# Recurrence of a decoder layer: another order of work on all engines, three pairs in flight, TensorE's program written out

## What is computed

```python
q = (x @ Wq).reshape(b, s, H, HD)
k = (x @ Wk).reshape(b, s, H, HD)
v = (x @ Wv).reshape(b, s, H, HD)
fg = jax.nn.sigmoid(x @ Wf + bf).reshape(b, s, H, HD)
...
state = state * gt[..., None] + vt[..., None] * kt[..., None, :]
out_t = jnp.einsum('bhij,bhj->bhi', state, qt)
```

## Time and profile before

| what | before |
|---|---|
| median of 3 runs | 2023.63 us (2019.81 to 2026.11) |
| the profiled execution: its own time | 2018.74 us |
| its span | 2016.6 us |
| TensorE busy in the span | 1864.5 us (92%) |
| VectorE, ScalarE, GpSimd busy | 1593.3, 1221.4, 390.4 us |
| mean granted clock of TensorE | 0.977 |
| the recurrence (to the first work of the next part) | about 755 us of the span |

### The profile page before, as it was taken

How to read it: one execution, slowest core, us unless ns; L and a number is a source line. 1 busy time by engine, 2 the same in 40 slices (tenths; PEclk the granted TensorE clock), 3 DMA queues, 4 the chain that set the end, 5 groups by cost and what they waited for, 6 DMA issues and landing times. The chain is left out here.

```text
span 2016.6 us, 71020 instructions
## 1 busy us (share of the span) xinstructions
PE 1864.5 (92%) x28151; PEld 1307.0 (65%) x28151; DVE 1593.3 (79%) x2870; ACT 1221.4 (61%) x2047; POOL 390.4 (19%) x516
## 2 busy tenths in 40 slices
PE   6999999999999977999999999999599988799798
PEld 4666666666666665888888888887344433344687
DVE  6777777777777775888888888887466799998897
ACT  4444554444445434777777777777355666688565
POOL 1111111211111121223232323232100222100121
PEclk9999999999999989999999999999699999999899
DMA  4001100110011001111111111110188788599574
GB/s 126 24 24 29 30 24 24 29 30 24 24 27 32 19 19 63 34 48 32 46 33 46 36 42 38 40 41 7 40 273 267 272 314 312 188 402 409 184 271 148
DMA packets 121324, 205.24 MB, mean 102 GB/s; under 512 B 44851, under 2 KB 98358, under 8 KB 121142
## 3 DMA queue, kind: packets, MB, share of 16 engines
q1 hardware_dynamic: 121142, 202.43, 29.4%
HBM read 108.01 MB, written 85.98 MB: 96 GB/s over the span
## 5 line engine op out<-in xcount | busy, mean ns | idle before, releaser
L1483 PE MATMUL ff_twin<-ff_xq,w_uh 128*128 (+1 forms) x1152 | 346.0, 382 | 40.0 <-DVE ff_top L1852 25.7
L1483 PEld LDWEIGHTS ff_twin<-ff_xq,w_uh 128*128 128x128 f16 x1152 | 110.4, 98 | 188.9 <-issue 43.2
L1483 PE MATMUL ff_twin<-ff_xq,w_ul 128*128 (+1 forms) x576 | 219.9, 382 | 0.0
L1214 DVE TENSOR_REDUCE mneg<-att_s 128x4 f32<-128x512 f32 x256 | 158.8, 683 | 31.3 <-PE att_s L977 31.3
L545 ACT ACTIVATE x<-rec_e,rec_hidden 128x512 f32<-128x512 f32 x256 | 155.8, 702 | 35.1 <-PE rec_e L380 35.1
L661 DVE TENSOR_TENSOR x<-rec_x,rec_until 128x512 f32<-128x512 f32 x256 | 158.7, 681 | 17.2 <-PE rec_x L364 17.2
L392 PE MATMUL rec_x<-x 32*32 32x64 f32 x8192 | 146.4, 219 | 14.9 <-DVE x L661 9.5
L392 PEld LDWEIGHTS rec_x<-x 32*32 32x32 f32 x8192 | 125.4, 107 | 51.4 <-issue 51.3
L288 POOL TENSOR_TENSOR rec_o<-rec_tmp 128x512 f32<-128x512 f32 x32 | 41.1, 1283 | 571.6 <-DVE rec_tmp L714 571.6
L1129 ACT ACTIVATE att_e<-att_s 128x512 f32<-128x512 f32 x256 | 132.2, 612 | 25.4 <-PE att_s L1011 25.4
L349 PE MATMUL rec_f<-rec_xT,w_rec 128*128 128x256 f32 x512 | 137.3, 402 | 0.8 <-ACT rec_v L527 0.8
(11 more groups left out here) (244 smaller groups left out, 4363.3 us busy)
## 6 DMA issues: line engine op xcount, KB each, us to landing
raw_scratch<-ff_out SPq DMA_DIRECT2D x32, 768.0 KB, 3.5
ff_in<-raw_scratch SPq DMA_DIRECT2D x32, 768.0 KB, 5.9
gate_scratch<-ff_out SPq DMA_DIRECT2D x28, 768.0 KB, 3.5
ff_in<-gate_scratch SPq DMA_DIRECT2D x28, 768.0 KB, 10.2
product_scratch<-ff_out SPq DMA_DIRECT2D x28, 768.0 KB, 9.7
ff_out<-product_scratch SPq DMA_DIRECT2D x28, 768.0 KB, 5.9
att_x<-in_x SPq DMA_DIRECT2D x32, 256.0 KB, 2.7
att_ctx<-in_ctx SPq DMA_DIRECT2D x32, 256.0 KB, 3.0
```

The lines of the kernel that those rows point to most:

```text
L1214: V.tensor_reduce(mneg[:, 4 * j:4 * j + 4], X[j].rearrange("p (h k) -> p h k", h=4), AX.X, ALU.max, negate=True).then_inc(q["s_taken"], 1)
L1483: m = T.matmul(bank_.rearrange("p (b n) -> p b n", b=BT), weights(wp, kc, a, c), tile[:, xp, :, kc], start=(i == 0), stop=(i == len(terms) ...
```

## The change

The recurrence's programs are written in another order on TensorE, ScalarE and VectorE. Each has now one `step` over the pairs prev, now and next_. TensorE's 34 steps are all written out, without a loop, so that its waits are on constants; ScalarE and VectorE keep a loop over two pairs. On TensorE `scores(., 0)` moves up into the step of its own pair, groups of small tiles stand next to each other (`inside` 0 and 1; `inside` 2 and half of `across_half`; a quarter part, `inside` 3, the other quarter part), `exponents` 3 and 4 stand together before the queries, and `value_gate` takes sequence 1 first. On VectorE `quarter_out` stands before `weighted(., 0)` and `half_out` behind it, and both `floor`s stand together. On ScalarE the queries' copies move behind the exponentials of k = 2, and the last two exponentials stand between the logarithm and its rounding. At the start the first `value_gate` waits for two weights, not for four; `sums` comes first on VectorE; the search for the scales is cut in three parts, of which `weigh_down` (which waits for three weight loads) stands before the first `split`. The functions keep their instructions; `across` is now `keys` and `queries`.

```diff
-    TURNS = 6
...
+        class Pair:
+            def __init__(self, j, c):
+                self.r, self.s, self.turn = 2 * j + c, c % 2, j + c // 2
+                self.first = isinstance(j, int) and c == 0
...
-                def products(p, n, s, so, front, back):
...
-                def pieces(p, s, before, front, back, more):
...
+                def step(at):
+                    prev, now, next_ = at(-1), at(0), at(1)
+                    if now:
+                        queries(now)
+                    if prev:
+                        scores(prev, 1)
+                    if now:
+                        keys(now, 0)
+                    if prev:
+                        inside(prev, 0)
+                        inside(prev, 1)
+                    if now:
+                        keys(now, 1)
+                        exponents(now, 0)
+                    if prev:
+                        inside(prev, 2)
+                        across_half(prev, 0)
+                    if now:
+                        exponents(now, 1)
+                    if next_:
+                        turn(next_)
+                    if now:
+                        exponents(now, 2)
+                    if prev:
+                        across_quarter(prev, 0)
+                        inside(prev, 3)
+                        across_quarter(prev, 1)
+                    if next_:
+                        value_gate(next_, 1)
+                    if prev:
+                        across_half(prev, 1)
+                    if next_:
+                        value_gate(next_, 0)
+                    if now:
+                        scores(now, 0)
+                        exponents(now, 3)
+                        exponents(now, 4)
                 pe.wait_ge(qw["ident_set"], 2)
...
-                with pe.Fori(0, (NP - 2) // TURNS) as j:
-                    for u in range(TURNS):
-                        p, s = TURNS * j + 1 + u, (1 + u) % 2
-                        pieces(p, s, TURNS // 2 * j + (1 + u) // 2, True, True, True)
-                        products(p + 1, p, 1 - s, s, True, True)
-                pieces(NP - 1, 1, (NP - 2) // 2, True, True, False)
-                products(NP, NP - 1, 0, 1, False, True)
-                pieces(NP, 0, NP // 2, False, True, False)
+                for p in range(-1, NP + 1):
+                    step(near(0, p))
...
+                def step(at):
+                    now, next_ = at(0), at(1)
+                    if now:
+                        keys_out(now)
+                        exps(now, 0)
+                    if next_:
+                        turned(next_)
+                    if now:
+                        exps(now, 1)
+                        exps(now, 2)
+                        queries_out(now)
+                    if next_:
+                        values_out(next_, 1)
+                        values_out(next_, 0)
+                        gate_exp(next_)
+                        gate_log(next_)
+                    if now:
+                        exps(now, 3)
+                        exps(now, 4)
+                    if next_:
+                        gate_high(next_)
...
+                def step(at):
+                    prev, now, next_ = at(-1), at(0), at(1)
+                    if prev:
+                        quarter_out(prev)
+                    if now:
+                        weighted(now, 0)
+                    if prev:
+                        half_out(prev)
+                    if next_:
+                        floor(next_, 1)
+                        floor(next_, 0)
+                        if next_.first:
+                            weigh_down()
+                    if now:
+                        scores_out(now, 0)
+                    if prev:
+                        total(prev)
+                    if now:
+                        scores_out(now, 1)
+                    if next_:
+                        split(next_)
+                        if next_.first:
+                            weigh_up()
+                    if now:
+                        weighted(now, 1)
                         for k in range(4):
-                            inside_out(n, so, k)
...
+                            inside_out(now, k)
+                        if now.first:
+                            weigh()```

TensorE, in the middle of the recurrence. First the place from the second scores to the first exponents. rec_x are the banks X, x with a source x is `inside`, rec_f the projections, rec_e `exponents`; a REGISTER_ALU or ISA row computes the number to wait for. Before:

```order
L364 MATMUL rec_x<-rec_qm,rec_kT 128x256 x8
L347 REGISTER_ALU
L349 MATMUL rec_f<-rec_xT,w_rec 128x256 x2
L386 REGISTER_ALU
L387 REGISTER_ALU
L392 MATMUL rec_x<-x 32x64 x32
L349 MATMUL rec_f<-rec_xT,w_rec 128x256 x2
L387 REGISTER_ALU
L392 MATMUL rec_x<-x 32x64 x32
L69 REGISTER_ALU
L380 MATMUL rec_e<-rec_nh,rec_sums_of 128x256
```

More of the change, by code:

```diff
@@ L165, in recurrence_block @@
         q = {n: sem("rec_" + n) for n in names}
-        names = "ident_set w_loaded bf_loaded raw_loaded rest_loaded part all chain weighed rounded turned copied high split cleared".split()
+        names = "ident_set w_loaded qk_loaded bf_loaded raw_loaded rest_loaded part all chain weighed rounded turned copied high split cleared".split()
         qw = {n: sem("weights_" + n) for n in names}
@@ L170, in blocks_of, with near, at @@
             return flat.rearrange("p (n q) -> p n q", q=QBLOCK)
-        def steps(eng, step):
-            step(0, 0, 0, True, False)
-            with eng.Fori(0, (NP - 2) // 2) as j:
-                for u in range(2):
-                    step(2 * j + 1 + u, (1 + u) % 2, j + u, True, True)
-            step(NP - 1, 1, (NP - 2) // 2, True, True)
-            step(NP, 0, NP // 2, False, True)
+        class Pair:
+            def __init__(self, j, c):
+                self.r, self.s, self.turn = 2 * j + c, c % 2, j + c // 2
+                self.first = isinstance(j, int) and c == 0
+        def near(j, u):
+            def at(k):
+                if isinstance(j, int) and not 0 <= u + k < NP:
+                    return None
+                return Pair(j, u + k)
+            return at
         def rows(j):
@@ L456, in pieces @@
-                def pieces(p, s, before, front, back, more):
-                    n, so = p - 1, 1 - s
-                    if back:
-                        inside(n, so, 0)
-                    if front:
-                        across(p, 1, F[0], 1, 1, q["k_made"])
-                    if back:
-                        inside(n, so, 1)
-                    if front:
-                        exponents(p, s, 0)
-                    if back:
-                        inside(n, so, 2)
-                    if front:
-                        exponents(p, s, 1)
-                    if more:
-                        turn(p + 1, so, before + s)
-                    if back:
-                        inside(n, so, 3)
-                    if front:
-                        exponents(p, s, 2)
-                    if back:
-                        across_half(n, 0)
-                    if more:
-                        value_gate(p + 1, 0)
-                    if back:
-                        across_half(n, 1)
-                    if front:
-                        exponents(p, s, 3)
-                    if back:
-                        across_quarter(n, 0)
-                    if front:
-                        exponents(p, s, 4)
-                    if back:
-                        across_quarter(n, 1)
-                    if more:
-                        value_gate(p + 1, 1)
@@ L517, in turned, with values_out @@
                 def turned(p):
-                    act.wait_ge(q["x_made"], p + 1)
+                    act.wait_ge(q["x_made"], p.r + 1)
                     A.activation(xT.rearrange("p k n -> p (k n)"), F[0][:], ACT.Copy).then_inc(q["xT_ready"], 1)
-                def step(p, s, before, front, back):
-                    if not front:
-                        return
-                    act.wait_ge(q["w_ready"], 2 * p) if not isinstance(p, int) or p else None
-                    for b in range(2):
-                        act.wait_ge(q["z_ready"], 2 * p + b + 1)
-                        A.activation(v[:, s, b * D:(b + 1) * D], F[1 - b][:, 0:D], ACT.Copy).then_inc(q["v_ready"], 1)
+                def values_out(p, b):
+                    if b == 1:
+                        wait_if(act, q["w_ready"], 2 * p.r - 2)
+                    act.wait_ge(q["z_ready"], 2 * p.r + 2 - b)
+                    A.activation(v[:, p.s, b * D:(b + 1) * D], F[1 - b][:, 0:D], ACT.Copy).then_inc(q["v_ready"], 1)
@@ new lines, in exps @@
+                def exps(p, k):
+                    if k == 0:
+                        wait_if(act, q["o_taken"], TAKES * (p.r - 1))
+                    act.wait_ge(q["e_made"], NE * p.r + k + 1)
+                    for asks, r in USES[k]:
```

(22 more changed lines are left out.)

255 lines of the change are left out of this document (111 added, 144 removed).

## The result

The changed kernel takes 2074.4 us (median of 4 runs, 2065.7 to 2077.9) against 2023.1 us: the ratio of the recorded runs is 1.0244 [1.0229, 1.0259] (the two medians alone give 1.0253), slower by 2.4%. The forecast was 2006 us. Its profiled execution, the shortest of the four, has a span of 2063.6 us, 47.0 us more than before.

What follows compares the result with a forecast made beforehand. TensorE was taken to bound the recurrence. A beat of 21.8 us saves 18.3 us and the start adds 1: -17.3 against 2018.7 gives 2001.4 us, and with the median 0.24% higher, 2006 us; range 1985 to 2022 us.

Steps and rivals of the forecast that it cites:

- The size of the stall per pair: TensorE's recurrence, small tiles closer together: instructions arrive late, 0.9 us per pair taken, between 0.25 and 1.9 or 2.6.
- rival B: Instruction fetching becomes the bound between the quarter parts: stall 1.9 or 2.6 us per pair, 2036 or 2057 us; chance 0.11.
- The share: Dense stretch: what is fetched ahead covers the same share as before, so 0.25/0.9 x 2.6 = 0.7 us of stall.
- The averaging: From `inside` 0 to the second quarter part, priced as one: 872 instructions, 12.2 us, in 9.6 us, short by 2.6.
- The packet price: TensorE's instruction queue: 239 instructions per packet, 3.3 us each, read from the last pair's 896 instructions.
- The clock: TensorE's lower clock level, tied to rival B's stretch between the quarter parts: 1.3 us each time.
- The beat: TensorE's interval per pair without added stall: 21.85 - 0.63 - 0.15 - 0.18 = 20.9 us on paper.
- The margins of 0.4 and 0.5 us: VectorE in the new order: ready 0.4 us before `across_half` and 0.5 us before the next masks, so no wait.
- rival C: A missed VectorE margin puts a new wait in place of the removed ones: +15 us, 2021 us; chance 0.14.
- The branches: TensorE's recurrence loop: writing it out removes four branch intervals, 10.6 us less, lower clock included.
- Start and end: Outside the recurrence's beat: first exponents 1 us later (0 to 3); end 0 us (-3 to +2).
- Rival A: Instruction fetching keeps up in the recurrence: stall stays 0.25 us, beat 21.15 us, 1987 us; chance 0.25.

Runs made afterwards that it cites:

- the probe: Kernel before plus, behind the last pair, 512 quarter-kind then 512 inside-kind matmuls of the program; 256 instructions cost 3.74 us (3.63 with narrow tiles).
- kernel 4: Changed kernel with `across_quarter` 0, `inside` 3 and `across_quarter` 1 spread apart, on TensorE alone: 2066.2 us, ratio 1.0215 to the kernel before.
- kernel 5: Against kernel 4, `quarter_out` of the pair before and the weighing change places on VectorE: 1991.3 us, ratio 0.9843 to the kernel before.
- Kernel 6: Changed kernel with the second piece of the keys placed between `inside` 0 and `inside` 1, nothing else: 2056.5 us, ratio 1.0158 to the kernel before.
- kernel 1: Kernel before, old order, with only TensorE's loop replaced by written-out code with constant waits: 2019.1 us, ratio 0.9978.
- kernel 9: Changed kernel with small tiles spread among wide products, `across_half` 0 behind the second quarter part, VectorE's order as in kernel 5: 1999.3 us, ratio 0.9865 to the kernel before.
- kernel 2: The probe: kernel before plus two written-out rows of small matmuls behind the last pair; 3.74 us per packet of 256 instructions.
- kernel 3: Kernel before plus, behind the last pair, a loop of 24 turns over one group of `inside` (128 instructions): 1.14 us per group.
- kernel 10: Against kernel 9, `across_half` 0 moved back behind `inside` 2: 1989.9 us, ratio 0.9832 to the kernel before.

## Why the prediction was wrong

**The size of the stall per pair is the step that failed** ("I take 0.9 us, near the first"). Measured are 47.3 us in 30 intervals, 1.6 us per pair. It lies in the prediction's own bounds (0.25 to 1.9 or 2.6 us) and just above the 1.5 us from which rival B decides. Two things in the working led to the low value.

- The share. The old order was short by 0.9 us on paper and showed 0.25, and I let the same share of 28% hold in the new one. Shown is 1.6 of 2.6. The other reading that the prediction had (a fixed 0.65 us covered, hence 1.9 us) comes nearer, but by the probe's prices the shortage is 12.7 - 9.6 = 3.1 us, of which 1.5 are covered, and this is neither 0.65 us nor 72%. How much is fetched ahead isn't shown.
- The averaging. I took the 9.6 us of small tiles as one stretch. Within it `across_quarter` 0, `inside` 3 and `across_quarter` 1 ask for 384 instructions in 2.4 us. That is 1.5 packets, 5.6 us by the probe. The 1.1 packets in 1.9 us of the old order, which I used as a reason for no stall, don't carry over to 1.5: 42 of the 47.3 us of issue lie there. Kernels 4 and 5, with these three apart, have 13.3 and 12.2 us of issue, but they don't tell the place from the average. Their stretch has `value_gate` 1 in it as well, 2.1 us more, and is short by only 1.0 us by the same sum. Kernel 6 keeps the stretch and its instructions, changes only the order in it, and has 38.0 us in place of 47.3, so the order inside the stretch does count.

The packet price was too low as well, but it decides less. It took 896 instructions for 3.75 packets; with 256 in each they are 3.5, at 3.6 us. For the dense stretch, 3.65 packets of 239 at 3.3 us are 12.2 us, 3.4 packets of 256 at 3.74 are 12.7 us.

**The clock was left out of the sum.** It stands in rival B only, at 1.3 us each time. It took about 47 us (what the account leaves), as much as the stalls. The earlier trace rows showed that a pause of 1.8 us can be followed by the lower clock; a forecast with stalls of 1 to 2 us had to price a fall behind a part of them. By the sum with the measured stall alone (30 x 20.67 + 47.3) the kernel would have been level: 619.4 + 47.3 = 666.7 against 670.8 us. The stalls eat the gain, and the clock makes the loss.

**The beat was right.** On paper 20.9 us, measured 20.67. Both removed waits are gone, and the exponents with them.

**VectorE was right.** The margins of 0.4 and 0.5 us held, with one wait of 0.6 us in 30 pairs; rival C didn't happen. How thin the second one is shows in kernel 4: with one call later on TensorE it was missed by 1.9 us per pair.

**The branches were half right.** They do give 10.6 us, but 7 us come back when the program is written out (kernel 1); why isn't shown. I had let all 10.6 us count and the ordinary stalls stay as they were.

**Start and end.** +0.9 us at the start (1 taken), +1.9 at the end (0 taken, +2 the bound).

**The signs.** The prediction named issue above 45 us as the sign of B; it is 47.3. B's mechanism and its place (the stretch between the two quarter parts) are what happened; I had given it 0.11. Rival A, by which the fetch keeps up, is refuted by the probe. A stall of the size that was to come, 2.29 us in front of quarter tiles, stood in the rows, but I used it only for the price of a packet.

**What stays open.** What sets the 3.74 us of a packet isn't shown; its transfer is a small part of it (1.9% of the DMA engines' time in the probe). It is also not shown why some stalls are followed by a low clock and others not. In the changed kernel 11 of the 14 stalls of L443 are (1.49 to 2.33 us long), and three (1.09 to 1.46 us) are not. But in the probe stalls of 1.76 us between tiles of 64 columns are not, in kernel 9 the clock falls behind tiles of 16 columns without a stall, and in kernel 4 it falls at 9 of 29 waits for VectorE of nearly the same length. And a stall of 1.81 us inside `inside` 3 of the changed kernel, at 335.69 us, has none behind it, as this window shows.

```profile
331.00:337.00 6.00, 4.19 (x215) 3.75 (x213) 0.88 (x2) 4.79 (x9) 0.64 (x1) 1.00 0.19 51
```

## What to carry to other kernels

Price small matmuls by the instructions that they need as well as by their time, and do it over every short run of them, not over the whole stretch: where a run asks for clearly more than one packet (here 384 instructions in 2.4 us, with 256 per 3.74 us), put a wide product into it. A stall of TensorE costs more than its length when the clock falls with it, so look at the granted clock of the wide products that follow. After such a spreading look at the other engines once more: here it brought a wait of 1.9 us per pair until VectorE's order was changed too.

## What the runs showed of the hardware

- Instructions of small tiles come 256 at a time, one packet per 3.74 us (mean 3.63 with 16 columns), while TensorE uses them up in 1.90 us (16 columns, clock 0.50) or 1.99 us (64 columns, clock 1.00) (kernel 2).
- A loop over 128 instructions ran 24 turns at 1.14 us each, branch included, with one packet fetched (kernel 3): four branches of the long loop cost 10.6 us, 24 of the short one next to nothing.
- The granted clock fell to 0.50 (of the two levels, 1.2 in place of 2.4 GHz) during or behind stalls by issue of 1.2 to 2.3 us in the changed kernel, and stayed there for 3.4 or 10.2 us though TensorE worked without a gap again. In the probe it was 0.50 with stalls of 1.56 to 2.11 us between tiles of 16 columns, and 1.00 with stalls of 1.76 us between tiles of 64 columns (kernel 2).
- It also fell without any idle time, behind 128 quarter and half tiles of 16 columns in a row (kernel 9, ten times), and not once there with one of the groups moved away (kernel 10). Of 1536 tiles of 64 columns in a row all but the first 5 us ran at 1.00 (kernel 3).
